# Third attention of a megakernel: softmax probabilities turned by VectorE and moved by GpSimd in place of TensorE's transposes

## What is computed

```python
def _L2_xattn_ref(Q, K, V, WQ, WK, WV, WO):
    q = jnp.einsum('bsd,hde->bhse', Q, WQ)
    k = jnp.einsum('btd,hde->bhte', K, WK)
    v = jnp.einsum('btd,hde->bhte', V, WV)
    scores = jnp.einsum('bhse,bhte->bhst', q, k) * 64 ** -0.5
    scores = jnp.where(jnp.tril(ones((1024, 77))), scores, -jnp.inf)
    wei = jax.nn.softmax(scores, axis=-1)
    out = jnp.einsum('bhst,bhte->bhse', wei, v)
    return out.transpose(0, 2, 1, 3).reshape(b, 1024, -1) @ WO

x = x + jnp.tanh(g_xattn[2]) * _L2_xattn_ref(_layernorm(x), ctx, ctx, WQ, WK, WV, WO)
```

## Time and profile before

| | us |
|---|---|
| timed runs, median of 3 | 2100.9 (2098.76 to 2102.35) |
| the profiled execution's own time | 2084.4 |
| its span, first to last instruction | 2082.6 |
| stage 4's attention, first subtraction to last addition | 779.7 to 943.6 |
| TensorE busy over the span | 1921.5 (92%) |
| VectorE busy | 1435.7 (69%) |
| ScalarE busy | 978.5 (47%) |
| GpSimd busy | 752.3 (36%) |

### The profile page before, as it was taken

The page is one execution under the profiler, slowest core; times in us unless marked ns, Lnnn a source line. Parts: engine busy times, 40 slices in busy tenths (PEclk is TensorE's granted clock), DMA queues, the critical chain, the costliest instruction groups (busy, mean ns, idle before and its releaser), DMA issues.

```text
span 2082.6 us, 33216 instructions
## 1 busy us (share of the span) xinstructions
PE 1921.5 (92%) x11797; PEld 1355.2 (65%) x11797; DVE 1435.7 (69%) x2676; ACT 978.5 (47%) x2079; POOL 752.3 (36%) x1145
## 2 busy tenths in 40 slices
PE   6997799696999988997878999999999999998999
PEld 3885799542699976883565666666675666655644
DVE  5775111467344457787867999999878999998755
ACT  5672333343111252226875555555545555555455
POOL 1002111000522200000006777777656777777500
PEclk9897899898999999998989999999999999999999
DMA  3702899502489960002002333333222333333201
GB/s 115 208 2 79 273 323 333 170 1 86 163 292 321 310 228 1 1 1 86 1 13 60 82 83 82 83 83 83 72 57 72 82 82 82 82 82 81 63 1 41
DMA packets 191184, 226.87 MB, mean 109 GB/s; under 512 B 28939, under 2 KB 167085, under 8 KB 191021
## 3 DMA queue, kind: packets, MB, share of 16 engines
q1 hardware_dynamic: 183725, 201.98, 33.0%
q0 software_dynamic: 7296, 22.78, 3.3%
HBM read 127.64 MB, written 29.91 MB: 76 GB/s over the span
## 4 chain that ended last, share of the span: by engine, by line
PE 45%; ACT 6%; DVE 3%; issue 1%; POOL 0%; ACTq 0%; DVEq 0%; POOLq 0%
PE ps L640 41%; ACT w_odd L1796 4%; PE ps L1214 2%; PE ps L1215 1%; ACT arena L1785 1%; PE ps L1106 0%; DVE w_odd L2532 0%; DVE small L2410 0%; POOL arena L1908 0%; ACT out_feat L1708 0%; PE ps L1115 0%; ACT xn_tok L1651 0%; DVE small L2522 0%; ACT out_feat L1714 0%; DVE arena L2380 0%
## 5 line engine op out<-in xcount | busy, mean ns | idle before, releaser
L1908 POOL COPY arena<-w_odd 32x512 f32<-32x512 f32 x1024 | 623.7, 609 | 254.4 <-DVE w_odd L2532 202.1
L640 PE MATMUL ps<-arena,w_odd 128*128 128x128 f32 (+4 forms) x2352 | 468.2, 441 | 3.0 <-DVE arena L2202 1.2
L640 PE MATMUL ps<-arena 128*64 128x256 f32 (+4 forms) x3248 | 392.3, 370 | 8.3 <-DVE arena L2333 4.4
L640 PEld LDWEIGHTS ps<-arena 128*64 128x64 f32 (+4 forms) x3248 | 258.9, 155 | 119.5 <-issue 22.6
L2532 DVE STREAM_TRANSPOSE w_odd<-w_odd 128x1024 f32<-128x1024 f32 x256 | 317.4, 1245 | 14.6 <-ACT w_odd L1796 3.0
L1796 ACT ACTIVATE w_odd<-ps,small 128x1101 f32<-128x1101 f32 x256 | 301.6, 1179 | 48.0 <-DVE small L2522 41.0
L640 PEld LDWEIGHTS ps<-arena,w_odd 128*128 128x128 f32 (+3 forms) x2352 | 286.3, 188 | 27.9 <-issue 18.7
L1781 ACT ACTIVATE arena<-ps 77x256 f32<-77x256 f32 x128 | 48.5, 379 | 295.4 <-PE ps L1215 295.4
L2522 DVE TENSOR_REDUCE small<-ps 128x1 f32<-128x1101 f32 x128 | 166.9, 1304 | 29.3 <-PE ps L640 28.1
L1893 POOL DMA_INDIRECT token_rows<-arena x62 | 59.8, 964 | 292.3 <-DVE arena L2223 292.3
L2523 DVE TENSOR_REDUCE small<-ps 128x1 f32<-128x1024 f32 x128 | 155.4, 1214 | 0.0
(11 more groups left out here) (398 smaller groups left out, 2909.8 us busy)
## 6 DMA issues: line engine op xcount, KB each, us to landing
arena<-w_odd SPq DMA_DIRECT2D x1024, 64.0 KB
w_odd<-in_s_w SPq DMA_DIRECT2D x32, 1024.0 KB, 7.4
w_odd<-in_s_wgu SPq DMA_DIRECT2D x30, 704.0 KB, 6.1
w_even<-in_s_w SPq DMA_DIRECT2D x15, 1024.0 KB, 7.3
arena<-expert_rows_in SPq DMA_DIRECT2D x62, 130.0 KB, 4.7
w_odd<-in_s_wd SPq DMA_DIRECT2D x30, 256.0 KB, 3.6
out_feat<-in_s_wgu SPq DMA_DIRECT2D x10, 704.0 KB, 5.9
expert_rows_in<-zero_row POOLq DMA_DIRECT2D x1, 5070.0 KB, 33.2
```

Of the source, the lines that this page charges most:

```text
L640: return pe.matmul(o, lhsT, rhs, start=start, stop=stop, **kw)
L1908: pool.tensor_copy(s6_d[u % 4][32 * j:32 * j + 32, :, 256 * i:256 * i + 256], s6_pm[u % 2][32 * i:32 * i + 32, :, 256 * j:256 * j + 256]). ...
```

## The change

In stage 4 the ten transposes of TensorE, ScalarE's copy and VectorE's two copies out of PSUM go. VectorE, after the multiplication, waits for it (`link`) and transposes the tile's `pr` slot in place in 32x32 blocks; the slot is widened from 1232 to 39 x 32 = 1248 columns (HCP). GpSimd then puts the 32x32 blocks where they belong in `pt`, with sixteen `tensor_copy` a tile: from partitions 32i to 32i+31 to partitions 32a to 32a+31, for each pair of i and a, ten pieces of 32 columns (nine for a = 3) at a stride of 128 columns on both sides. Each copy raises the new semaphore `at_mv` by one. GpSimd starts a tile at `at_p`, and waits until the product two tiles earlier has read the `pt` slot (`at_o`). TensorE's product waits for 16 more of `at_mv`, and VectorE's subtraction into a `pr` slot (L2013) waits for the copies of tile t-3 where it waited for its transposes. Stage 0 stays as it is.

```diff
--- before.py
+++ after.py
@@ -121,6 +121,9 @@
         s4_vo = cut(AR, 4928, B, NF, D)
         SC4 = 4928 + 5120
         s4_kt, s4_vt = (cut(OT[:, :, :].rearrange("p c n -> p (c n)"), at, 8, B * C) for at in (0, 1232))
+        HCP = 39 * 32
+        s4_pr = cut(AR, SC4, 3, HCP)
+        s4_pt = cut(AR, SC4 + 3 * HCP, 2, NF * P)
         at_max, at_sum, at_rec = cut(small, 0, 2, H), cut(small, 32, 2, H), cut(small, 64, 2, H)
         s0_nm = cut(small, 0, 2, 4, 4)
         WHOLE = 3
@@ -305,6 +308,7 @@
         c6_mm, c6_sb = sem("c6_mm"), sem("c6_sb")
         a6_s, a6_mx, a6_p, a6_rb, o6_sd = sem("a6_s"), sem("a6_mx"), sem("a6_p"), sem("a6_rb"), sem("o6_sd")
         r6_mm, r6_act, r6_dve = sem("r6_mm"), sem("r6_act"), sem("r6_dve")
+        at_mv = sem("at_mv")
         t6_done, copied6, t6_base = t5_c, t5_f, NT
         moved6, moved_base = vo_out, 32
         z6_in, g6_sb, x6_b = sem("z6_in"), sem("g6_sb"), sem("x6_b")
@@ -706,9 +710,9 @@
             def attention(s, score, fill=None):
 
                 t0 = NT * at_no[s]
-                SCR, region, VO = (WE, SC0, s0_vo) if s == 0 else (AR, SC4, s4_vo)
-                pr = cut(SCR, region, 3, HC)
-                pt = cut(SCR, region + 3 * HC, 2, NF * P)
+                pr, pt, VO = cut(WE, SC0, 3, HC), cut(WE, SC0 + 3 * HC, 2, NF * P), s0_vo
+                if s == 4:
+                    pr, pt, VO = s4_pr, s4_pt, s4_vo
                 if s == 4:
                     vo_copied(pe, B * H - 2)
                     vo_copied(pe, B * H - 1)
@@ -717,7 +721,7 @@
                         score(t)
                     if fill:
                         fill(t)
-                    if 2 <= t < NT + 2:
+                    if s == 0 and 2 <= t < NT + 2:
                         u = t - 2
                         pe.wait_ge(at_p, t0 + u + 1)
                         if u >= 1:
@@ -736,8 +740,11 @@
                             pe.wait_ge(at_add, t0 + u)
                         if s == 0 and u == 8:
                             pe.wait_ge(vo_in, 64)
-                        pe.wait_ge(at_pta, t0 + u + 1)
-                        pe.wait_ge(at_ptv, t0 + u + 1)
+                        if s == 0:
+                            pe.wait_ge(at_pta, u + 1)
+                            pe.wait_ge(at_ptv, u + 1)
+                        else:
+                            pe.wait_ge(at_mv, 16 * (u + 1))
                         if s == 4 and u == 4:
                             pe.wait_ge(q5_n, 1)
                             mm(PS[:, 7, D:D + 2], ones[:, :], s5_n[:, 0:2]).then_inc(q5_s, 1)
@@ -1461,9 +1468,7 @@
 
             def attention(s, ahead=None, behind=None):
                 t0 = NT * at_no[s]
-                SCR, region = (WE, SC0) if s == 0 else (AR, SC4)
-                pr = cut(SCR, region, 3, HC)
-                pt = cut(SCR, region + 3 * HC, 2, NF * P)
+                pr, pt = cut(WE, SC0, 3, HC), cut(WE, SC0 + 3 * HC, 2, NF * P)
                 for t in range(NT + 2):
                     if ahead:
                         ahead(t)
@@ -1484,10 +1489,10 @@
                         act.activation(hc, hc, ACT.Exp).then_inc(at_exp, 1)
                     elif t < NT:
                         act.wait_ge(at_sub, t0 + t + 1)
-                        act.activation(pr[:, t % 3], pr[:, t % 3], ACT.Exp, scale=DH ** -0.5).then_inc(at_exp, 1)
+                        act.activation(s4_pr[:, t % 3, 0:HC], s4_pr[:, t % 3, 0:HC], ACT.Exp, scale=DH ** -0.5).then_inc(at_exp, 1)
                     if behind:
                         behind(t)
-                    if t >= 2:
+                    if s == 0 and t >= 2:
                         u = t - 2
                         act.wait_ge(at_tr, t0 + u + 1)
                         if u >= 2:
@@ -1896,6 +1901,18 @@
             for s in stages:
                 if s in (1, 3):
                     expert_tiles(s)
+                if s == 4:
+                    for u in range(NT):
+                        pool.wait_ge(at_p, NT + u + 1)
+                        if u >= 2:
+                            pool.wait_ge(at_o, NT + u - 1)
+                        for a in range(4):
+                            nf = NF if a < 3 else NF - 1
+                            for i in range(4):
+                                src = s4_pr[32 * i:32 * i + 32, u % 3, 32 * a:32 * a + 32]
+                                src = bass.AP(tensor=src.tensor, offset=src.offset, ap=[src.ap[0], [P, nf], [1, 32]])
+                                dst = s4_pt[32 * a:32 * a + 32, u % 2].rearrange("p (f q) -> p f q", f=NF)[:, 0:nf, 32 * i:32 * i + 32]
+                                pool.tensor_copy(dst, src).then_inc(at_mv, 1)
                 if s == 6:
                     pool.wait_ge(g6_sb, 1)
                     pool.wait_ge(ln_xn, NT * (xn_no[ln_no[6]] + 1))
@@ -1968,9 +1985,7 @@
 
             def attention(s, gate, fill=None):
                 t0 = NT * at_no[s]
-                SCR, region = (WE, SC0) if s == 0 else (AR, SC4)
-                pr = cut(SCR, region, 3, HC)
-                pt = cut(SCR, region + 3 * HC, 2, NF * P)
+                pr, pt = (cut(WE, SC0, 3, HC), cut(WE, SC0 + 3 * HC, 2, NF * P)) if s == 0 else (s4_pr, s4_pt)
                 for t in range(NT + 4):
                     if s == 0 and t == 4:
                         dve.wait_ge(x0_b, 1)
@@ -2009,11 +2024,11 @@
                         sc = PS[:, 0:4, 0:GC].rearrange("p g (h c) -> p g h c", h=4)
                         link(dve.tensor_reduce(at_max[:, q].rearrange("p (g h) -> p g h", g=4), sc, AX.X, ALU.max))
                         if t >= 3:
-                            dve.wait_ge(at_tr, t0 + t - 2)
-                        dve.tensor_tensor(pr[:, t % 3].rearrange("p (g h c) -> p g h c", g=4, h=4), sc,
+                            dve.wait_ge(at_mv, 16 * (t - 2))
+                        dve.tensor_tensor(pr[:, t % 3, 0:HC].rearrange("p (g h c) -> p g h c", g=4, h=4), sc,
                                           at_max[:, q].rearrange("p (g h) -> p g h", g=4).unsqueeze(3).broadcast_to([P, 4, 4, C]),
                                           ALU.subtract).then_inc(at_sub, 1)
-                    if 2 <= t < NT + 2:
+                    if s == 0 and 2 <= t < NT + 2:
                         u = t - 2
                         dve.wait_ge(at_tr, t0 + u + 1)
                         if u >= 2:
@@ -2023,7 +2038,7 @@
                     if 1 <= t <= NT:
                         u = t - 1
                         q = u % 2
-                        hc = pr[:, u % 3].rearrange("p (h c) -> p h c", h=H)
+                        hc = pr[:, u % 3, 0:HC].rearrange("p (h c) -> p h c", h=H)
                         if s == 0:
                             n = 1 if u >= WHOLE else 4
                             dve.wait_ge(at_exp, u + 1)
@@ -2035,7 +2050,11 @@
                             dve.wait_ge(at_exp, t0 + u + 1)
                             link(dve.tensor_reduce(at_sum[:, q], hc, AX.X, ALU.add))
                         link(dve.reciprocal(at_rec[:, q], at_sum[:, q]))
-                        dve.tensor_tensor(hc, hc, at_rec[:, q].unsqueeze(2).broadcast_to([P, H, C]), ALU.mult).then_inc(at_p, 1)
+                        last = dve.tensor_tensor(hc, hc, at_rec[:, q].unsqueeze(2).broadcast_to([P, H, C]), ALU.mult)
+                        if s == 4:
+                            link(last)
+                            last = dve.transpose(pr[:, u % 3], pr[:, u % 3])
+                        last.then_inc(at_p, 1)
                     if s == 4:
                         whole_numbers(t)
                     if s == 0:
```

## The result

| | before | after |
|---|---|---|
| timed runs, median of 16 each, us | 2099.91 (2095.05 to 2103.29) | 2109.01 (2103.63 to 2113.09) |
| ratio after / before, 95% interval | | 1.0042 (1.0032 to 1.0051) |
| span of the profiled execution, us | 2082.6 | 2108.6 |
| stage 4, first maximum to end of last addition, us | 165.37 | 174.40 |

The change makes the kernel 9.1 us slower. The two profiled spans differ by 26 us, and that must not be read as the change: the first maximum of stage 4 stands at 778.27 us before and at 794.45 after, so 16.2 us come from ahead of the stage, where the code is the same. Behind the stage the two need nearly the same time (1139.0 us before, 1139.7 after).

A forecast was written before the change was run, and what follows sets the result against it. TensorE was taken to bound a tile, by 2.21 us over VectorE. After the change GpSimd's queue ends the stage 8.2 us later and the clock adds 1.8: +10.0, a median of 2110.9 us, range 2098 to 2140.

The forecast's parts named there:

- GpSimd's queue: Stage 4: GpSimd's copies, late start and waits end the last addition at 951.8 us, +8.2 us.
- TensorE's gain is not collected: Stage 4: TensorE saves 1.09 us a tile, but VectorE pays back its gain in the weight passes.
- Copies: GpSimd's sixteen copies a tile in stage 4: 8.1 us, between bounds of 4.3 and 10.6 us.
- The port: Stage 4's multiplication reading two SBUF tensors beside GpSimd's copies: 1.1 us lost on GpSimd, 0.25 us on VectorE.
- weight pass: One of six VectorE passes preparing stage 5's weights during stage 4: 1.22 to 1.29 us, plus 1.1 on GpSimd.
- the second sum: Second of two VectorE sums of 2.28 us in the weight preparation, early in stage 4.
- The clock in the tail: End of stage 4: TensorE's waits lower the granted clock, 1.8 us taken from between 0 and 4.4.
- twelve tiles of 8.7 us: Check by VectorE alone: twelve stage 4 tiles, with weight passes, put tile 15's maximum at 919.2 us.
- Rival 1: Stage 4 is VectorE bound, gain and loss cancel: +3.6 or about 0, time 2099 to 2105 us, chance 0.17.
- Rivals 2 to 4: In stage 4: cheap copies, 2095 to 2097 us, chance 0.06; dear copies, +20 up, 0.19; VectorE shut out, +90, 0.02.

The follow-up runs named there:

- rec_psum: The changed kernel with stage 4's reciprocals in PSUM, so the multiplication reads one SBUF tensor; ratio to before 1.0015, stage 168.53 us.
- warm: The changed kernel with 24, 14 and 26 identity transposes ahead of TensorE's last three waits for copies; ratio to before 1.0049, stage 175.44 us.
- turn_beside: The kernel before plus VectorE's wait and a 1248-column transpose of a region nobody reads, TensorE's transposes kept; ratio to before 1.0040, stage 176.04 us.
- best: split_rec with the six weight passes moved from VectorE to GpSimd; ratio to before 0.9962, stage 163.18 us.
- split_rec: The changed kernel with the edits of split and rec_psum together; ratio to before 1.0008, stage 167.45 us.
- split: The changed kernel with four of a tile's sixteen copies moved from GpSimd to ScalarE; ratio to before 0.9990, stage 165.23 us.
- few_before: The kernel before with five of the six weight passes cut from 2048 to 8 columns, for timing only; ratio to before 0.9999, stage 164.67 us.
- twenty: The changed kernel with four more GpSimd copies a tile, repeated into a region nobody reads; ratio to before 1.0162, stage 198.66 us.

## Why the prediction was right, step by step

Forecast +10.0 us, measured +9.1; the mechanism was the one named, GpSimd's queue with VectorE close behind it. That the sum came out within 0.9 us is in part luck, as the errors below have both signs.

- **TensorE's gain is not collected.** Right. Tile 15's maximum starts 141.68 us after the first, before 141.71 (the earlier trace rows less 778.27); forecast was 0.8 earlier. Transpose on VectorE: 1.48 forecast, 1.478 measured. Tile 15 turned 2.6 us later than it was ready before; forecast 2.2.
- **Copies.** 0.455 and 0.430 us forecast for 320 and 288 elements, 0.445 to 0.447 and 0.422 measured; a train 8.1, measured 7.96. So pieces of 32 elements cost no more than the line between the two rows gives.
- **The port.** On GpSimd 1.1 us for a multiplication, shown by rec_psum: 1.11 in the mean. For a weight pass 1.1 was too much: 0.91 and 0.92, in two experiments. On VectorE 0.25 us was too much: 0.11 in the mean for the multiplication, 0.17 for a pass. So VectorE gets in behind a copy more cheaply than L2495 did.
- **GpSimd's queue.** 153.5 us from first copy to last forecast (946.8 - 793.3), 961.94 - 809.54 = 152.4 measured. The forecast has one gap of 0.80 us, the trace three: the second sum holds tile 2's transpose back too, and the masked scores of tile 8 that of tile 7. Those 1.6 us are outweighed by the prices of the passes and of the tiles, each a little too high. It was to be the later by 4.6 us; by the rows above it was by 961.94 - 958.7 = 3.2.
- **The clock in the tail.** 1.8 us taken from between 0 and 4.4; the last product took 6.24 against 4.5. That this is the clock warm shows.
- **Left out.** Tile 8 has 24 score products of 6.2 us in all; VectorE waits 2.69 us for them (867.72), and the prediction's twelve tiles of 8.7 us have no such term. The maximum of tile 15 still came within 0.8 us of the forecast, because VectorE's waits beside GpSimd were priced about 2.2 us too high in all (12 x 0.14 + 6 x 0.08): luck. GpSimd loses no more than its gap of 0.80. And the start: the scores of tile 3 took 7.12 us at a clock of 0.90 in the first 35 us. The prediction allowed a low clock only at the end. In after it costs next to nothing, since VectorE is at its second sum meanwhile and waits only 0.19 us for these scores (821.65). It cost 3.5 us in turn_beside and 4.1 in best, by the two kernels that filled the waits, and had a large part in the misses of both expectations; that of split_rec failed in the same stretch, but there nothing was filled. In these three traces the scores of tile 1 were slow before any edit had acted, so the clock at the start is not simply a price of the change.
- **Rival 1** (VectorE bound) gave +3.6: that is rec_psum, 3.2 us above before, the kernel in which GpSimd isn't delayed. **Rivals 2 to 4** needed a copy of 0.35 us or less, or of 0.66, or a multiplication that waits for the whole train; the rows show 0.50 from start to start and a wait of 0.11.

What isn't settled: why the scores of tile 1 take 4.41 us in some traces and up to 7.44 in others after the same wait; why the product of tile 13 runs at the lower clock in all kernels with a transpose on VectorE except warm, where the wait ahead of it was filled, but not that of tile 14; and how the gains of split, rec_psum and the moved passes share out by themselves, since each also moves TensorE's waits.

## What to carry to other kernels

A step handed to an idle engine is free only while that engine's whole time for a tile, with what its neighbours on the port take from it, stays below the bound's, and its full serial time comes once more at the end of the stage. Where VectorE works on two SBUF tensors beside GpSimd, put one of them in PSUM: that took 5.9 us off this stage. And where TensorE waits a few us at a time, price its next products at both levels of the granted clock, at the stage's start as well as at its end, and don't put a slow group down to an edit before checking that the edit had acted by then.

## What the runs showed of the hardware

- After waits of 2.6 to 5.2 us sixteen score products took 6.1 to 7.4 us in place of 4.4 at the start of the stage in eleven of the thirteen kernels, before included; the other two had these waits filled. Twenty products of 256 columns took 6.2 to 7.5 in place of 4.5 somewhere in ten of them, not in before, few_before and warm. Not each wait has this effect: the one of 3.01 us ahead of a score group was followed by 4.41 us fourteen times and by 6.10 to 7.44 nine times. Identity transposes in the waits (24 in 2.78 us) brought back 4.4 and 4.5 where they were put.
- In twenty a copy on GpSimd that reads and writes the same partitions as the one before it starts 0.40 us after it; one that reads other partitions and writes the same starts 0.50 us after it, as one that changes both does. So other source partitions are enough for the 0.50. Other destination partitions alone weren't tried.
- GpSimd needs 1.89 to 1.97 us for a two-operation pass over 2048 columns, but 5.4 for the pass with one operation (a subtraction of a constant; 5.36 to 5.38 us, twice), where VectorE takes 1.2 to 1.3 for either. Timeline of GpSimd in best:

```profile
893.50 1.89 POOL L1942 TENSOR_SCALAR w_odd<-w_odd 128x2048 f32<-128x2048 f32 x1
895.86 6.02 POOL L1932 COPY arena<-arena 32x320 f32<-32x320 f32 x12 [0.47 <-POOL w_odd L1942]
901.96 5.38 POOL L1945 TENSOR_SCALAR w_odd<-w_odd 128x2048 f32<-128x2048 f32 x1
```
